# One tile of edges per block group in a sparse attention, with V sums added tile by tile and two heads of the V product on ScalarE

## The reference

```python
q = (z @ Wq + bq).reshape(L, H, D)
k = (z @ Wk + bk).reshape(L, H, D)
v = (z @ Wv + bv).reshape(L, H, D)
scores = jnp.einsum('ehd,ehd->eh', q[row], k[col]) * scale + bias
m = jax.ops.segment_max(scores, row, num_segments=L)
p = jnp.exp(scores - m[row])
ssum = jax.ops.segment_sum(p, row, num_segments=L)
alpha = p / ssum[row]
out = jax.ops.segment_sum(alpha[:, :, None] * v[col], row, num_segments=L)
return out.reshape(L, C) @ Wo + bo
```

## Time and profile before

| | us |
|---|---|
| median of 3 runs (3580.56 to 3590.44) | 3586.35 |
| time of the profiled execution | 3575.87 |
| its span | 3574.1 |
| K gathers, first to last start (608) | 841.4 to 1607.1 |
| K products on DVE, first to last start | 853.9 to 1616.2 |
| V gathers after the first 16 (592) | 1639.5 to 2381.3 |
| V products on DVE, first to last start | 1638.5 to 2385.1 |
| mean granted TensorE clock | 0.897 |

### The profile page before, as it was taken

How to read it: one execution, slowest core, us unless ns; L and a number is a source line. 1 busy time by engine, 2 the same in 40 slices (tenths; PEclk the granted TensorE clock), 3 DMA queues, 4 the chain that set the end, 5 groups by cost and what they waited for, 6 DMA issues and landing times. The chain is left out here.

```text
span 3574.1 us, 57773 instructions
## 1 busy us (share of the span) xinstructions
PE 2822.7 (79%) x12010; PEld 1811.5 (51%) x12011; DVE 2576.7 (72%) x5150; ACT 1472.9 (41%) x4642; POOL 2200.7 (62%) x2242
## 2 busy tenths in 40 slices
PE   7898888844888888887888887866999997599960
PEld 5555555522333333334655555645787785366630
DVE  6766666625899999998888887885656552477764
ACT  6322322213565556665545454533333332144420
POOL 2477777776777777776777777752222210088866
PEclk9788888867999999998999999987999999799985
DMA  3444444444777777776777777774222222633339
GB/s 108 170 161 142 148 157 136 150 142 151 210 208 210 209 209 210 209 209 185 214 214 213 213 210 215 212 227 152 79 73 83 73 71 95 215 109 112 112 120 320
DMA packets 234218, 594.77 MB, mean 166 GB/s; under 512 B 50865, under 2 KB 59954, under 8 KB 229170
## 3 DMA queue, kind: packets, MB, share of 16 engines
q0 software_dynamic: 127104, 362.93, 35.9%
q1 hardware_dynamic: 102898, 222.79, 17.7%
q10 hardware_dynamic: 4032, 7.34, 0.6%
HBM read 500.74 MB, written 92.15 MB: 166 GB/s over the span
## 5 line engine op out<-in xcount | busy, mean ns | idle before, releaser
L1214 PE MATMUL at_bank<-product,v_hot 128*128 128x260 f32 x2432 | 629.8, 404 | 117.8 <-DVE product L970 110.9
L1168 PE MATMUL at_bank<-wide,hot_t 128*128 x1216 | 614.1, 627 | 124.6 <-ACT hot_t L1036 65.5
L803 POOL DMA_INDIRECT fetched<-t_k,at_index x608 | 581.7, 957 | 192.5 <-issue 133.7
L812 POOL DMA_INDIRECT fetched<-t_v,at_index x608 | 577.2, 949 | 197.0 <-issue 133.1
L348 POOL DMA_INDIRECT records<-staged,address x544 | 533.1, 980 | 265.0 <-issue 165.3
L1214 PEld LDWEIGHTS at_bank<-product,v_hot 128*128 128x128 f32 x2432 | 443.1, 195 | 299.0 <-issue 136.1
L886 DVE TENSOR_TENSOR product<-at_bank,fetched 128x512 f32<-128x512 f32 x608 | 413.7, 682 | 52.4 <-issue 33.6
L970 DVE TENSOR_TENSOR product<-fetched,at_turn 128x520 f32<-128x520 f32 x608 | 405.8, 689 | 62.3 <-DMA fetched<-t_v,at_index 31.2
L1168 PEld LDWEIGHTS at_bank<-wide,hot_t 128*128 128x128 f32 x1216 | 206.6, 194 | 377.7 <-issue 332.0
L617 PE MATMUL qkv_prod<-wide 128*128 128x512 f32 x768 | 378.0, 653 | 0.0
L843 DVE TENSOR_REDUCE raw_score<-product 128x7 f32<-128x448 f32 x608 | 348.2, 575 | 0.0
(11 more groups left out here) (292 smaller groups left out, 4330.2 us busy)
## 6 DMA issues: line engine op xcount, KB each, us to landing
row_bc<-in_src SPq DMA_DIRECT2D x34, 1024.0 KB, 4.7
by_slot<-m_y SPq DMA_DIRECT2D x72, 256.0 KB, 2.0
low_bc<-low_row SPq DMA_DIRECT2D x34, 512.0 KB, 5.5
fetched<-t_k,at_index POOLq DMA_INDIRECT x608, 3.7
fetched<-t_v,at_index POOLq DMA_INDIRECT x608, 3.8
records<-staged,address POOLq DMA_INDIRECT x544, 2.1
t_v<-wide SPq DMA_DIRECT2D x32, 260.0 KB
wide<-in_x SPq DMA_DIRECT2D x32, 256.0 KB, 2.9
```

The lines of the kernel that those rows point to most:

```text
L803: eng.indirect_dma_start(fetched[:, n % SLOTS, 0:C], None, k, bass.IndirectOffsetOnAxis(index[:, t:t + 1], 0)).then_inc(s_row[n % SLOTS], 16)
L812: eng.indirect_dma_start(fetched[:, n % SLOTS, :], None, v, bass.IndirectOffsetOnAxis(index[:, t:t + 1], 0)).then_inc(s_row[n % SLOTS], 16)
L1168: nc.tensor.matmul(q_edge[u % 4][:, :], hot_t[:, g % 2, u % BATCH * P:(u % BATCH + 1) * P], q_sb[:, bass.ds(at, 1), :].rearrange("p a c -> ...
L1214: last = nc.tensor.matmul(bank[g % 2 * 2 + n][:, 0:HALF], hot[:, u % 4, :], product[:, u % 4, n * HALF:(n + 1) * HALF], start=first, stop= ...
```

## The change

`GROUP` goes from 2 to 1, so that each block is rounded up to one tile of 128 edges: the bound on tiles becomes 69632/128 + 32 = 576. With `PAIR` kept at 2, `RANGE_TILES` becomes 36 and `TURNS` 18; the loop still has 8 rounds, and one straight turn less stands behind it.

Since every tile may now belong to another block, PE reads a block number for each tile in the K pass, and in the V pass each tile is a sum of its own: PE writes it to one of three pairs of PSUM banks (`start=True, stop=True` for each tile), and DVE adds it with one instruction of 520 elements over both banks, two tiles later (`LAG`), with a block number read each time. DVE multiplies only the first 6 heads; ACT does the last two with a Copy each, scaled by a weight per partition from `act_weight`, which ACT copies from PSUM once per turn (`keep_weights`). Gathers of V, PE and the transposes of the next weights wait for this too (`r_act_scaled`).

```diff
-GROUP = 2
+GROUP = 1
...
+V_DVE = HEADS - 2
...
-    PAIR = GROUP
+    PAIR = 2
...
-    G2 = TURN // GROUP
+    LAG = 2
...
+        act_weight = sb("act_weight", [P, 2, PAIR, RANGES, HEADS - V_DVE])
...
-        bank = [part.enter_context(nc.psum_tensor(f"at_bank{n}", [P, C], F32)) for n in range(4)]
-        q_edge = bank
-        low_ps = [part.enter_context(nc.psum_tensor(f"at_low{n}", [P, C], F32)) for n in range(2)]
+        pair = [part.enter_context(nc.psum_tensor(f"at_pair{n}", [P, 2, C], F32)) for n in range(LAG + 1)]
+        q_edge = [pair[n // 2][:, n % 2, :] for n in range(4)]
+        low_ps = [pair[2][:, n, :] for n in range(2)]
...
-            with eng.Fori(0, (TURNS - 3) // 2) as j:
+            with eng.Fori(0, (TURNS - 2) // 2) as j:
                 for b in range(2):
                     body(j * 2 + (b + 1), 1 - b, True)
-            body(TURNS - 2, 1, True)
-            body(TURNS - 1, 0, False)
+            body(LAST, 1, False)
...
                     r_scaled.wait(eng, m, u - SLOTS)
+                    r_act_scaled.wait(eng, m, u - SLOTS)
...
-            def add(m, g):
-                at = eng.value_load(groups[0:1, bass.ds(group_at(back_of(m), g), 1)], min_val=0, max_val=BLOCKS - 1)
-                r_tile.wait(eng, m, (g + 1) * GROUP - 1)
-                r_total.wait(eng, m, g - 1)
-                to = total[:, bass.ds(at, 1), :].rearrange("p a w -> p (a w)")
-                for n in range(2):
-                    mine = to[:, n * HALF:(n + 1) * HALF]
-                    ins = nc.vector.tensor_tensor(mine, bank[g % 2 * 2 + n][:, 0:HALF], mine, ALU.add)
-                ins.then_inc(r_total.sem(g), 1)
+            def add(m, u):
+                at = eng.value_load(groups[0:1, bass.ds(tile_at(back_of(m), u), 1)], min_val=0, max_val=BLOCKS - 1)
+                r_tile.wait(eng, m, u)
+                r_total.wait(eng, m, u - 1)
+                to = total[:, bass.ds(at, 1), :].rearrange("p a (n w) -> p (a n) w", n=2)
+                nc.vector.tensor_tensor(to, pair[u % 3][:, :, 0:HALF], to, ALU.add).then_inc(r_total.sem(u), 1)
...
                     nc.vector.tensor_tensor(
-                        product[:, u % 4, :].rearrange("p (h w) -> p h w", h=HEADS),
-                        fetched[:, u % SLOTS, :].rearrange("p (h w) -> p h w", h=HEADS),
-                        turn_ps[b][:, at:at + HEADS].unsqueeze(2).broadcast_to([P, HEADS, VHEAD]), ALU.mult
+                        product[:, u % 4, 0:V_DVE * VHEAD].rearrange("p (h w) -> p h w", h=V_DVE),
+                        fetched[:, u % SLOTS, 0:V_DVE * VHEAD].rearrange("p (h w) -> p h w", h=V_DVE),
+                        turn_ps[b][:, at:at + V_DVE].unsqueeze(2).broadcast_to([P, V_DVE, VHEAD]), ALU.mult
                     ).then_inc(r_scaled.sem(u), 1)
-                    if u >= GROUP and u % GROUP == GROUP - 1:
-                        add(m, u // GROUP - 1)
-                    elif u == GROUP - 1 and not (isinstance(m, int) and m == 0):
-                        add(m - 1, G2 - 1)
+                    if u >= LAG:
+                        add(m, u - LAG)
+                    elif not (isinstance(m, int) and m == 0):
+                        add(m - 1, TURN + u - LAG)
...
+            def keep_weights(m, b):
+                r_weight.wait(eng, m, 0)
+                by_tile = turn_ps[b][:, 0:CHUNK].rearrange("p (j c h) -> p j c h", j=PAIR, c=RANGES)
+                nc.scalar.copy(act_weight[:, b, :, :, :], by_tile[:, :, :, V_DVE:]).then_inc(r_act_weight.sem(0), 1)
...
+                    if u == 0:
+                        r_act_weight.wait(eng, m, 0)
+                    eng.wait_ge(s_row[u % SLOTS], fetch_count(m, u) + v_from)
+                    for h in range(V_DVE, HEADS):
+                        ins = nc.scalar.activation(product[:, u % 4, h * VHEAD:(h + 1) * VHEAD],
+                                                   fetched[:, u % SLOTS, h * VHEAD:(h + 1) * VHEAD], ACT.Copy,
+                                                   scale=act_weight[:, b, u % PAIR, u // PAIR, h - V_DVE:h - V_DVE + 1])
+                    ins.then_inc(r_act_scaled.sem(u), 1)
...
-                    if u % GROUP == 0:
-                        at = eng.value_load(groups[0:1, bass.ds(group_at(i, u // GROUP), 1)], min_val=0, max_val=BLOCKS - 1)
+                    at = eng.value_load(groups[0:1, bass.ds(tile_at(i, u), 1)], min_val=0, max_val=BLOCKS - 1)
...
-                    g, first, final = u // GROUP, u % GROUP == 0, u % GROUP == GROUP - 1
                     r_v_hot.wait(eng, m, u)
-                    if first:
-                        r_total.wait(eng, m, g - 2)
+                    if u < LAG:
+                        r_total.wait(eng, m, u - LAG)
+                    elif u > LAG:
+                        r_total.wait(eng, m, u - LAG - 1)
                     r_scaled.wait(eng, m, u)
+                    r_act_scaled.wait(eng, m, u)
                     for n in range(2):
-                        last = nc.tensor.matmul(bank[g % 2 * 2 + n][:, 0:HALF], hot[:, u % 4, :],
-                                                product[:, u % 4, n * HALF:(n + 1) * HALF], start=first, stop=final)
+                        last = nc.tensor.matmul(pair[u % 3][:, n, 0:HALF], hot[:, u % 4, :],
+                                                product[:, u % 4, n * HALF:(n + 1) * HALF], start=True, stop=True)
```

More of the change, by code:

```diff
@@ L647, in attention @@
     PARTS = 8
-    assert TILES == TURN * TURNS and RANGE_TILES == PAIR * TURNS and TURNS % 2 == 1
+    LAST = TURNS - 1
+    assert TILES == TURN * TURNS and RANGE_TILES == PAIR * TURNS and TURNS % 2 == 0 and GROUP == 1
     assert TILES % SLOTS == 0 and TURN % SLOTS == 0
@@ L725, in attention @@
         s_chain, s_ends, s_carry, s_carried, s_clear = (sem(f"a_{n}") for n in ("chain", "ends", "carry", "carried", "clear"))
-        r_v_away, r_v_hot, r_scaled, r_tile = (one(f"v_{n}", TURN) for n in ("away", "hot", "scaled", "tile"))
-        r_total = one("v_total", G2)
-        r_back, r_sub, r_exp, r_weight = (one(f"v_{n}", 1) for n in ("back", "sub", "exp", "weight"))
+        r_v_away, r_v_hot, r_scaled, r_act_scaled, r_tile, r_total = (
+            one(f"v_{n}", TURN) for n in ("away", "hot", "scaled", "act_scaled", "tile", "total"))
+        r_back, r_sub, r_exp, r_weight, r_act_weight = (one(f"v_{n}", 1) for n in ("back", "sub", "exp", "weight", "act_weight"))
         s_fix, s_norm, s_share = (sem(f"v_{n}") for n in ("fix", "norm", "share"))
@@ L885, in key_turn @@
                     r_last.wait(eng, i, u - 4)
-                    nc.vector.tensor_tensor(product[:, u % 4, 0:C], q_edge[u % 4][:, :], fetched[:, u % SLOTS, 0:C],
+                    nc.vector.tensor_tensor(product[:, u % 4, 0:C], q_edge[u % 4], fetched[:, u % SLOTS, 0:C],
                                             ALU.mult).then_inc(r_product.sem(u), 1)
@@ L982, in _ @@
             value_turns(eng, value_turn)
-            add(last, G2 - 1)
-            r_total.wait(eng, last, G2 - 1)
+            for u in range(TURN - LAG, TURN):
+                add(LAST, u)
+            r_total.wait(eng, LAST, TURN - 1)
             st = Steps(eng, s_share)
@@ L1002, in _ @@
         def _(eng):
-            for r in (r_away, r_hot_t, r_last, r_keyx, r_keys, r_kept, r_v_away, r_v_hot, r_back, r_exp):
+            for r in (r_away, r_hot_t, r_last, r_keyx, r_keys, r_kept, r_v_away, r_v_hot, r_act_scaled, r_act_weight, r_back, r_exp):
                 r.start(eng)
@@ L1029, in distance @@
                 r_edge.wait(eng, i, (g - 1) * BATCH - 1)
-                nc.scalar.activation(hot_t[:, g % 2, :], low_ps[g % 2][:, :], ACT.Abs, bias=neg_p[:, :]
+                nc.scalar.activation(hot_t[:, g % 2, :], low_ps[g % 2], ACT.Abs, bias=neg_p[:, :]
                                      ).then_inc(r_away.sem(g), 1)
@@ L1097, in _ @@
             exponentials(0, 0)
+            def keep_weights(m, b):
+                r_weight.wait(eng, m, 0)
+                by_tile = turn_ps[b][:, 0:CHUNK].rearrange("p (j c h) -> p j c h", j=PAIR, c=RANGES)
+                nc.scalar.copy(act_weight[:, b, :, :, :], by_tile[:, :, :, V_DVE:]).then_inc(r_act_weight.sem(0), 1)
+            keep_weights(0, 0)
             def value_turn(m, b, more):
@@ L1110, in value_turn @@
                                          ).then_inc(r_v_hot.sem(u), 1)
+                    if u == 0:
+                        r_act_weight.wait(eng, m, 0)
+                    eng.wait_ge(s_row[u % SLOTS], fetch_count(m, u) + v_from)
[4 more added lines that the diff above has]
+                    ins.then_inc(r_act_scaled.sem(u), 1)
                     if more and u == 18:
                         exponentials(m + 1, 1 - b)
+                    if more and u == 28:
+                        keep_weights(m + 1, 1 - b)
             value_turns(eng, value_turn)
@@ L1167, in key_turn @@
                     r_product.wait(eng, i, u - 4)
```

(7 more changed lines are left out.)

8 lines of the change are left out of this document (2 added, 6 removed).

## The result

The kernel after the change takes 3538.78 us (median of 4 runs, 3535.48 to 3541.78) against 3585.17 for the kernel before (4 runs): a ratio of 0.987 (0.9853 to 0.9887), 46.4 us less. The forecast was 65 less. So the direction was right, but the time is that of rival (a), which had put V at 735 to 750 us and the total at 3540 to 3555: the measured values lie at its lower edge.

The account below looks back on a forecast made before the run. POOL's gathers were taken to bound V, DVE narrowly K. Terms of -37.5 (K), +2 (PE's loads), -31 (V) and +1.4 (small parts) gave -65 us: 3521 from the median 3586.35, range 3503 to 3560.

Parts of the forecast that it names:

- rival (a): V held by DVE or its sequencer at up to 1.30 us per tile; total 3540 to 3555; chance 0.23.
- Fewer tiles: 32 tiles fewer per pass: K 37.5 us less by DVE's pace, V's POOL floor 40.2 us less, at 701.6.
- Block number per tile on PE in K: 272 more loads on PE in K, mostly covered: 2 us, between nothing and 136 us.
- Rival (b): PE's loads show in K and take half of the K gain; total 3540; chance 0.05.
- DVE in V: DVE's product and two-bank addition at 1.17 us per tile; V products' stretch 716 us, 31 us less.
- Block number per tile on DVE's sequencer: In V the sequencer needs about 1.1 us per tile, under the engine's 1.17, and runs ahead: no cost.
- ACT in V: Two new Copies per tile on ACT at 0.25 to 0.33 us each: no cost, upper end 55 us.
- POOL's second wait: One more semaphore wait on POOL between V gathers: no cost.
- V gathers more than 1.30 us apart: Sign in V that the forecast is wrong and V is held by DVE or its sequencer.
- (c): DVE's sequencer doesn't run ahead in V: near 1.45 us per tile, V +88, total about 3640; chance 0.07.

Follow-up runs that it names:

- k_fixed: The changed kernel without the block number read on PE in K, a constant block instead; 3536.0 us, ratio 0.9863 to the kernel before.
- v_fixed: The changed kernel without the block number read on DVE in V, a constant block instead; 3515.6 us, ratio 0.9812 to the kernel before.
- no_assert: The changed kernel with block numbers read without the run-time bounds check on DVE and PE; 3517.9 us, ratio 0.9819 to the kernel before.
- k_heads66: The changed kernel without bounds checks, DVE reducing six heads and ACT two on every K tile; repeated on another chip 3507.4 us, ratio 0.9789 to before.
- dve8_no_assert: The changed kernel with all eight heads of the V product on DVE and no bounds checks; repeated on another chip 3561.2 us, ratio 0.9935 to before.
- b_act_heads: The kernel before with only two heads of the V product moved to ACT; repeated on another chip 3587.5 us, ratio 1.0013 to before.
- b_no_assert: The kernel before with only the bounds checks left out; repeated on another chip 3584.5 us, ratio 1.0009 to before.

## Why the prediction was off in size

- **Fewer tiles.** Right in both passes. K's loop pace was forecast at 1.28; with PE's loads out of the way (k_fixed) a round takes 81.8 us, 1.279 per tile, and 724.3 is 38 us under 762.4, against a term of -37.5. In V, v_fixed brought the gathers behind the first 16 to 701.4 us, against a floor of 701.6.
- **Block number per tile on PE in K ("I take 2 us").** Mis-sized: 5 to 7.5 us. That PE is late was foreseen; the waits for it rose from 6.9 us in the loop to 8.8 and fell to 0.5 without the load. Rival (b) asked for over 15 us of such waits and didn't say over which stretch: it is 8.8 in the loop, and 15.8 over the whole pass, where the kernel before has 12.6. Rival (b)'s price, half of the K gain, did not come.
- **DVE in V ("I take the middle, 716").** The durations were right: 551 ns for the product (555 forecast), 698 for the addition over two banks (about 690), 0.61 from start to start. With `settle`, the data path is 1.08 + 3.2/64 = 1.13 us per tile, under my 1.17. I had started from the busy time per tile, 1.034; from start to start the rows give 0.605 + 0.335 + 0.05 = 0.99, and 0.136 on top is 1.13. So this term was 8 us too high: V without the read took 708.2, not 716, and that hid a part of the miss in the next one.
- **Block number per tile on DVE's sequencer ("I take nothing here").** This is the step that failed. V took 734.9 instead of 711.4 (no check) or 708.2 (no read), so the check alone was worth 24 us and the whole term, put at nothing, was +27. I had the sequencer at "about 1.1, less than the engine's 1.17". Two things were wrong in that comparison. The pace that the sequencer sets in the loop is 1.115 us, as forecast, but between `settle` operations the data path needs only 1.08: my 1.17 had `settle` spread over all tiles, and the sequencer can't spread it. And I drew the running ahead from one place of the trace of before, where there was one read per two tiles. With a read per tile the lead is used up within four tiles in the stretch shown, and there is none behind two of the three `settle` operations of a turn and behind the jump, where the addition comes 1.01 and 1.18 us behind its product. That is near the 1.03 in the earlier trace rows; it needed to be counted at each of those places. Why there is no lead behind these two operations and one behind the third is open.
- **ACT in V.** Right: 333 ns per Copy, and v_fixed and no_assert reach POOL's pace with ACT's work unchanged. By the rule of the Trainium skill ("ScalarE: Activation LUTs", What ACT_TABLE_LOAD costs) for an ACTIVATE with one per-partition operand, 280 ns plus 0.833 per element, the estimate is 334 ns, and the trace agrees.
- **POOL's second wait.** Right: with DVE out of the way (v_fixed) gathers stand 1.255 us apart with it.
- **Rivals.** (a) came true, by its sequencer part alone; the other resources that it named are unchanged in v_fixed. The sign that was set for it, V gathers more than 1.30 us apart, was missed by a little: 1.294. (c), no running ahead at all, did not come true: V took 734.9/575 = 1.28 us per tile, not 1.45.

The sum with the measured terms is -38 + 7.5 for K and -12 for V, so -42; the medians say -46, and the 4 us between are within what the unchanged stages vary. That the total stayed inside the stated range is no proof of the sum: the range was drawn to hold rival (a) as well.

## What to carry to other kernels

An engine has two budgets per tile, its data path's and its sequencer's. Comparing the two per tile is enough only where the sequencer has a lead; here the sequencer's full chain showed behind the jump and behind two of three larger operations. The register load took 0.31 us of that chain and its bounds check another 0.30, so where the value is bounded by construction, leave the check out before moving arithmetic. And a part that gives nothing alone (two heads to ACT: +0.1%) can be what another part needs (43 us), so it is tried beside that part.

## What was not expected of the hardware

Four kernels first ran on a chip on which the kernel before took 4241.17 us, 18% more than elsewhere. The gathers' duration there is the same, but the engines have gaps. POOL in order of time in V, k_heads66 on that chip:

```profile
2213.50 0.95 POOL L811 DMA_INDIRECT fetched<-t_v,at_index  x1 [0.30 <-issue]
2217.42 0.94 POOL L811 DMA_INDIRECT fetched<-t_v,at_index  x1 [2.97 <-DVE product L967]
```

Before 59 of its 575 later V gathers POOL stood idle for over 2 us, 190 us in all, often 7 or 8 gathers apart, and V took 936 us instead of 714. There k_heads66 came to 0.9735 (0.9675 to 0.9795), dve8_no_assert to 0.9756 (0.9677 to 0.9836), b_act_heads to 1.0017 (0.9951 to 1.0082) and b_no_assert to 4245.4 us (4173 to 4251). In the V loop the gathers stand 1.62 to 1.65 us apart in all four, whichever engine has how much to do, so those runs don't tell six heads from eight. The two with 64 gathers fewer are 91 to 106 us shorter there. The profiles name waits between the engines in both directions and no first cause, and the mean granted TensorE clock was 0.83 there against 0.90. What makes the gaps is open; it was not tried.
